# Cross attention on one Trainium2 core: four key tiles of each softmax denominator added by accumulating DMAs instead of by TensorE

## What is computed

```python
q = hidden_state @ Wq + bq                     # (b, 8, 4, l, 32)
k = encoder_hidden_state @ Wk + bk             # (b, 8, s, 32)
v = encoder_hidden_state @ Wv + bv
scores = einsum('bkgld,bksd->bkgls', q, k) * scale + mask
attn = softmax(scores, axis=-1)
out = einsum('bkgls,bksd->bkgld', attn, v)
x = out @ Wo + bo + hidden_state
return (x - mean(x)) * rsqrt(var(x) + EPS) * gamma + beta
```

## Time and profile before

| | |
|---|---|
| median of 3 runs | 4496.38 us (4492.47 to 4497.11) |
| profiled execution | 4489.78 us |
| its span, first to last instruction | 4488.1 us |
| busy in the span | TensorE 95%, VectorE 60%, GpSimd 59%, ScalarE 50% |
| mean granted TensorE clock | 0.973 |
| `attend` | about 853 to 4023 us |

### The profile page before, as it was taken

The page is one execution under the profiler, slowest core; times in us unless marked ns, Lnnn a source line. Parts: engine busy times, 40 slices in busy tenths (PEclk is TensorE's granted clock), DMA queues, the critical chain, the costliest instruction groups (busy, mean ns, idle before and its releaser), DMA issues. The chain is left out here.

```text
span 4488.1 us, 82254 instructions
## 1 busy us (share of the span) xinstructions
PE 4262.9 (95%) x26418; PEld 2461.2 (55%) x26418; DVE 2677.2 (60%) x4874; ACT 2259.2 (50%) x3861; POOL 2654.7 (59%) x857
## 2 busy tenths in 40 slices
PE   8999997999999999999999999999999999987887
PEld 7998885444444444444444444444444444436766
DVE  3344443766666666666666666666666666625555
ACT  2222111366666666666666666666666666651110
POOL 1111111377767777777677767776777777762444
PEclk9999998799999999999999999999999999998999
DMA  4445554211211212121221112112211211016553
GB/s 169 145 152 190 202 195 165 68 35 35 77 39 36 64 36 52 36 64 36 49 60 43 37 47 68 36 35 50 67 35 36 77 40 35 21 45 180 157 154 117
DMA packets 253832, 357.34 MB, mean 80 GB/s; under 512 B 123232, under 2 KB 160480, under 8 KB 253408
## 3 DMA queue, kind: packets, MB, share of 16 engines
q1 hardware_dynamic: 227920, 272.37, 22.1%
q0 software_dynamic: 21504, 70.80, 4.1%
q10 hardware_dynamic: 3984, 8.91, 0.5%
HBM read 262.35 MB, written 88.60 MB: 78 GB/s over the span
## 5 line engine op out<-in xcount | busy, mean ns | idle before, releaser
L871 ACT ACTIVATE weights<-logit 128x512 f32<-128x512 f32 (+1 forms) x3328 | 1974.4, 598 | 1156.2 <-PE logit L714 1139.2
L652 POOL TENSOR_TENSOR sum_pool<-sum_pool,weights 128x2048 f32<-128x2048 f32 x448 | 2057.1, 4592 | 303.1 <-ACT weights L871 287.5
L714 PE MATMUL logit<-q_sb,k_sb 98*128 98x512 f32 (+1 forms) x3328 | 1447.2, 439 | 35.7 <-issue 32.7
L825 DVE CUSTOM_DVE_ANT_0 masked_row<-score,mask_max,half_max 128x804 f32<-128x804 f32 x1024 | 1080.0, 1055 | 582.3 <-PE score L687 516.8
L825 DVE CUSTOM_DVE_ANT_0 masked_row<-score,mask_max 128x800 f32<-128x800 f32 x1024 | 1013.9, 990 | 420.3 <-PE score L687 306.4
L687 PE MATMUL score<-k_sb,q_sb 96*128 96x400 f32 (+1 forms) x4096 | 1158.9, 365 | 28.9 <-DVE half_max L825 10.2
L714 PEld LDWEIGHTS logit<-q_sb,k_sb 98*128 98x128 f32 (+1 forms) x3328 | 615.2, 185 | 759.6 <-ACT weights L871 636.3
L724 PE MATMUL mixed<-weights,v_sb 128*32 128x256 f32 (+1 forms) x10752 | 1001.2, 444 | 0.0
L687 PEld LDWEIGHTS score<-k_sb,q_sb 96*128 96x128 f32 x4096 | 754.2, 194 | 395.9 <-issue 154.9
L652 POOL TENSOR_TENSOR sum_pool<-weights 128x2048 f32<-128x2048 f32 x64 | 294.5, 4601 | 601.5 <-ACT weights L871 601.5
L724 PEld LDWEIGHTS mixed<-weights,v_sb 128*32 128x32 f32 x10752 | 212.1, 108 | 414.1 <-issue 396.5
(11 more groups left out here) (85 smaller groups left out, 2912.3 us busy)
## 6 DMA issues: line engine op xcount, KB each, us to landing
q_sb<-q_parts SPq DMA_DIRECT2D x192, 256.0 KB, 4.0
k_sb<-k_parts SPq DMA_DIRECT2D x192, 200.1 KB, 5.2
rows<-in_ctx SPq DMA_DIRECT2D x26, 1024.0 KB, 5.2
landing<-in_mask_Bx1xSxS_ff SPq DMA_DIRECT2D x32, 800.5 KB, 5.2
mask_max<-in_mask_Bx1xSxS_ff SPq DMA_DIRECT2D x32, 800.5 KB, 6.4
rows<-in_x SPq DMA_DIRECT2D x16, 1024.0 KB, 5.4
q_parts<-o_hi POOLq DMA_DIRECT2D x64, 256.0 KB, 2.3
q_parts<-o_lo POOLq DMA_DIRECT2D x64, 256.0 KB, 3.0
```

Of the source, the lines that this page charges most:

```text
L652: nc.gpsimd.tensor_tensor(sum_pool[s % 2][:], first[:], weights[buffer(s, st)][:], ALU.add).then_inc(pool_added, 1)
L714: last = nc.tensor.matmul(bank[0:w, :], k_sb[s][:, keys], q_sb[s][:, h, :], start=True, stop=not masked, skip_group_check=masked)
L825: nc.vector.tensor_tensor_reduce(masked_row[j][:].rearrange("p (c s) -> p c s", c=2), score[j][:, :, 0:w], mask_max[:, lt, s0:s0 + 2 * w]. ...
L871: nc.scalar.activation(weights[buffer(s, st)][0:w, h, :], logit[h % 2][0:w, :], ACT.Exp).then_inc(exp_done, 1)
```

## The change

GpSimd still adds its nine tiles. The four REST tiles are added into one of them by DMA: tile 2's buffer is the base, and tiles 5, 11 and 12 are added into it by `pool.dma_start(..., accum_op=ALU.add)`, issued by GpSimd in `add_rest` and counted by `rest_added`. The DMA of tile 5 is issued before the addition of tile 7 (n = 4), that of tile 11 before the addition of tile 10 (n = 7), so GpSimd waits there for tile 11's exponentials first; that of tile 12 after the addition of tile 10. Each waits for the one before it to land, the first for the mix of tile 2. `total` is gone. `denominators` sums `sum_pool`, waits for the third DMA, and sums the base, in one visit at tile 2 of the following step.

`sum_pool` has one buffer, so the first addition of a step waits until the step before's visit is over. Tile 2 has two buffers of its own, tiles 5, 11 and 12 have a ring of two. ScalarE waits for the DMA that read a buffer (tile 2: for the visit that read it) before it writes it anew. `EARLY` goes from 3 to 1, so two more slices of Wo, 512 KB each, are fetched by the output stage.

```diff
-EARLY = 3
+EARLY = 1
...
+    BASES = 2
...
+    ADD_REST = {4: 1, NPOOL - 1: 2}
...
-        sum_pool = [sb(f"sum_pool{i}", [P, G, LQ]) for i in range(2)]
+        weights = [sb(f"weights{i}", [P, G, LQ]) for i in range(BASES + sum(RINGS))]
+        sum_pool = sb("sum_pool", [P, G, LQ])
...
                 if n == 0:
-                    pool.wait_ge(denom_done, step + 1)
+                    pool.wait_ge(denom_done, step + 2)
...
+            def add_rest(quad, s, k):
+
+                step, st = quad * QUAD + s, REST[k]
+                w = min(P, S - st * P)
+                pool.wait_ge(exp_done, quad * (QUAD * ST * G) + (s * ST + st + 1) * G)
+                if k == 1:
+                    pool.wait_ge(mix_done, quad * (QUAD * ST) + (s * ST + REST[0] + 1 + MIX0))
+                else:
+                    pool.wait_ge(rest_added, step * 48 + 16 * (k - 1))
+                pool.sem_inc(pool_seen, 1)
+                pool.dma_start(weights[buffer(s, REST[0])][0:w], weights[buffer(s, st)][0:w], accum_op=ALU.add).then_inc(rest_added, 16)
...
                         for n in range(NPOOL):
+                            if n in ADD_REST:
+                                add_rest(a * (KVH // QUAD) + q, s, ADD_REST[n])
                             add(a * (KVH // QUAD) + q, s, n)
+                        add_rest(a * (KVH // QUAD) + q, s, 3)
...
-            def total(quad, tile):
-
-                s, st = tile // ST % QUAD, tile % ST
-                if st == REST[0] and not (isinstance(quad, int) and quad * QUAD + s == 0):
-                    pe.wait_ge(denom_copied, quad * QUAD + s)
-                pe.wait_ge(exp_done, quad * (QUAD * ST * G) + (tile + 1) * G)
-                w = min(P, S - st * P)
-                sum_heads(denom, ones[0:w, :], weights[buffer(s, st)], w, st == REST[0], False)
-
-            def denominators(step, par):
+            def denominators(quad, s):
+                step = quad * QUAD + s
+                if not (isinstance(step, int) and step == 0):
+                    pe.wait_ge(denom_copied, step)
                 pe.wait_ge(pool_added, step * NPOOL + NPOOL)
-                sum_heads(denom, ones[:], sum_pool[par], P, False, True).then_inc(denom_done, 1)
+                sum_heads(denom, ones[:], sum_pool, P, True, False)
+                pe.wait_ge(rest_added, step * 48 + 48)
+                sum_heads(denom, ones[:], weights[buffer(s % QUAD, REST[0])], P, False, True).then_inc(denom_done, 1)
...
                                 if st == SUMS_AT and not (first and s == 0):
-                                    denominators(quad * QUAD + (s - 1), (s - 1) % 2)
-                                if (tile - LAG) % ST in REST and not (first and tile < LAG):
-                                    total(quad, tile - LAG)
+                                    denominators(quad, s - 1)
```

More of the change, by code:

```diff
@@ L445, in ring @@
     def ring(st):
-        return (POOL, RINGS[0], 0) if st in POOL else (REST, RINGS[1], RINGS[0])
+        return (POOL, RINGS[0], BASES) if st in POOL else (REST[1:], RINGS[1], BASES + RINGS[0])
     def buffer(s, st):
+        if st == REST[0]:
+            return s % BASES
         tiles, size, first = ring(st)
@@ L454, in tile_before @@
     def tile_before(s, st):
+        if st == REST[0]:
+            return s - BASES, st
         tiles, size, _ = ring(st)
@@ L477, in attend @@
         parts_t = sb("parts_t", [NROW, 2, P], F32R)
-        weights = [sb(f"weights{i}", [P, G, LQ]) for i in range(sum(RINGS))]
-        sum_pool = [sb(f"sum_pool{i}", [P, G, LQ]) for i in range(2)]
+        weights = [sb(f"weights{i}", [P, G, LQ]) for i in range(BASES + sum(RINGS))]
+        sum_pool = sb("sum_pool", [P, G, LQ])
         ones = sb("ones", [P, HD])
@@ L510, in attend @@
         pool_added = sem("pool_added")
+        rest_added = sem("rest_added")
+        pool_seen = sem("pool_seen")
         mix_done = sem("mix_done")
@@ L650, in add @@
                     pool.wait_ge(pool_added, step * NPOOL + n)
-                    first = sum_pool[s % 2]
-                nc.gpsimd.tensor_tensor(sum_pool[s % 2][:], first[:], weights[buffer(s, st)][:], ALU.add).then_inc(pool_added, 1)
+                    first = sum_pool
+                nc.gpsimd.tensor_tensor(sum_pool[:], first[:], weights[buffer(s, st)][:], ALU.add).then_inc(pool_added, 1)
+            def add_rest(quad, s, k):
[8 more added lines that the diff above has]
+                pool.dma_start(weights[buffer(s, REST[0])][0:w], weights[buffer(s, st)][0:w], accum_op=ALU.add).then_inc(rest_added, 16)
             pool.wait_ge(flag_done, 1)
@@ L789, in steps @@
                 for tile in range(QUAD * ST - LAG, QUAD * ST):
-                    total(NQUAD - 1, tile)
                     mix(NQUAD - 1, tile)
-                denominators(NSTEP - 1, 1)
+                denominators(NQUAD - 1, QUAD - 1)
             pe.wait_ge(flag_done, 1)
@@ L863, in exponents @@
                 if h == 0 and not (isinstance(quad, int) and quad == 0 and before < 0):
-                    act.wait_ge(mix_done, quad * (QUAD * ST) + (before * ST + old + 1 + MIX0))
-                    if old in POOL:
-                        act.wait_ge(pool_added, quad * (QUAD * NPOOL) + (before * NPOOL + max(POOL.index(old), 1)))
+                    if st == REST[0]:
+                        act.wait_ge(denom_done, quad * QUAD + (before + 1 + 2))
+                    else:
+                        act.wait_ge(mix_done, quad * (QUAD * ST) + (before * ST + old + 1 + MIX0))
+                        if old in POOL:
+                            act.wait_ge(pool_added, quad * (QUAD * NPOOL) + (before * NPOOL + max(POOL.index(old), 1)))
+                        else:
+                            act.wait_ge(rest_added, quad * (QUAD * 48) + (before * 48 + 16 * REST.index(old)))
                 act.wait_ge(logit_done, quad * (QUAD * ST * G) + (n + 1 + LOGITS0))
```

## The result

The changed kernel takes 4953.70 us (median of 4 runs, 4952.83 to 4957.47) against 4496.43: a ratio of 1.102, 95% interval 1.100 to 1.104. It is slower, as forecast, but by 457 us and not 124, and outside the range.

What follows compares the result with a forecast made beforehand. TensorE, busy 95% of the span, was taken as the bound. 50 steps at +3.0 us (+152), 13 loop turns (-36), stage end (+5) and Wo (+3) gave +124, so 4620 us; range 4280 to 4850.

Steps and rivals of the forecast that it cites:

- TensorE saves 3.46 us a step: TensorE's matmuls: four denominator visits removed save 4.36 us, a second run of 8 matmuls costs 0.90, net 3.46 a step.
- The DMAs are issued at 19.2 and so on: GpSimd's queue, from tile 6's addition: tile 11's DMA issued at 19.2 us; TensorE wants tile 12's landed at 28.8.
- An accumulate takes twice the moving time: Accumulating DMAs: two reads double the moving part, so landing takes 7.1 us for tile 11 and 5.0 for tile 12.
- What DMA 11 meets: Tile 11's DMA beside the q and k loads: 5.5 us of movement becomes 10.5 if the two share evenly.
- DMA 12, 65 rows: Tile 12's accumulating DMA: 5 rows for each engine, 1.7 us as a copy, doubled, landing after 5.0 us alone.
- What it meets: Tile 12's DMA beside other traffic: 0.9 us for what is left of the loads and for v, if all pass in turn.
- Alone: Tile 12's DMA without the loads: issued at 26.4 us, landing at 31.4, which is 2.6 late.
- The lateness of 5.0 us: TensorE's wait for tile 12's DMA at tile 2: between 2.6 late alone and 8.5 with all in turn, taken as 5.0.
- The stall costs 1.5 us more by the clock: TensorE behind a stall of 5 us: the clock falls to 0.50, as behind a loop turn, losing 1.5 us.
- The 13 steps at a turn: Turns of the quad loop: GpSimd has 4.3 us more room, slow clock already paid; -3.46 + 0.7, 13 times: -36 us.
- The end of the stage and Wo: Stage end: tile 12's DMA behind the last addition, +5 us; output stage: 1 MB more of Wo, +3 us.
- My rival of 8.5 us late: Tile 2 wait: all DMAs pass in turn, or a slower accumulate; 8.5 us late, 4840 us; chance 0.20.

## Why the prediction was right in direction and wrong in size

- *TensorE saves 3.46 us a step.* 3.07: the count of the visits was right, and 0.4 goes to the wait for VectorE at tile 1. The statement that VectorE has room and doesn't take the place of the bound was true of the mean and not of that one place. Over the run it is 205 us, not 221.
- *The DMAs are issued at 19.2 and so on.* DMA 11 at 19.4; an accumulating issue takes 0.87 us of GpSimd, not 0.6, but only some of it in the chain. TensorE wants DMA 12 at 29.5, not 28.8.
- *An accumulate takes twice the moving time: DMA 11 7.1 us alone.* 7.0 without the loads. Right. The Trainium skill, Collectives: The Full Stack, on why ReduceScatter is half of AllGather, lays the half rate of an adding transfer to its two reads. DMA 5, which the loads of q, k and v don't reach, nearly agrees: its packets take 0.33 us as plain copies and 0.64 as accumulates, and its moving 3.2 and 5.4.
- *What DMA 11 meets.* It was down 9.6 us after its issue, as GpSimd sees it (29.0 less 19.4), where my middle value was 9.1. Right.
- *DMA 12, 65 rows: 5 rows for each engine, 1.7 us, doubled, lands after 5.0 alone, and 0.4 of 0.9 us more for what it meets: 5.4.* **This is the step that failed.** It took 9.0 us (2090.82 to 2099.83), and it is both terms that were wrong. *What it meets:* in 46 of 64 steps it stands behind the loads, which DMA 11 had held up, and moves its first byte after 4.4 us, not after 1.4: 3.0 us where I had 0.4. Its moving then takes 3.8, near my 3.4. *Alone:* 8.5 and not 5.0, because it starts at once but moves at half rate; rows 0 to 63 against 32 to 95 showed it, 7.9 to 4.4. I divided rows by engines and took the rate of transfers that span all the partitions. In the changed kernel this second term shows in few steps, above all those at the turns and the last ones, and it is why taking the loads away doesn't make DMA 12 land sooner. How much rows in the middle would gain beside the loads no run shows.
- *The lateness of 5.0 us.* 8.5 in the mean of the 50 steps that are not at a turn. DMA 12 took 3.6 more than forecast; its late issue (0.6) and TensorE's later wish for it (0.7) cancel.
- *The stall costs 1.5 us more by the clock.* The second term mis-sized: 2.3 in the mean of these 50 steps, up to 2.9. The stall of 8.5 us is over three times that of the loop's turn from which I took the price; in the step shown the clock is still at 0.50 some 6 us after work has begun again.
- *The 13 steps at a turn: 0.7 us of wait and no clock.* 5.3 of wait and 1.9 of clock. The wait is 3.2 less than in the other steps, where I allowed 4.3 less; in these steps DMA 12 moves at about half rate. And the clock, up again after the turn, falls once more behind the stall.
- *The end of the stage and Wo.* At the end of the stage TensorE waits 6.5 us for `sum_pool` and 8.2 for the DMA, where it waited 2.6: 12 us more, and I had 5. From the end of attention on the kernels take 465 and 464 us; `EARLY` costs nothing that can be seen, where I had 3.

Of the 333 us that the forecast was short, 50 steps make 215 (3.5 and 0.8 each), the turns 84, the saving 16 and the end of the stage 7, less 3 for Wo: 319.

The step shown adds up: 45.88 without DMAs, 8.54 of stall and 2.92 of clock are 57.34; the trace has 57.24 (2042.59 to 2099.83). Over the run this kernel takes 665 us more than the one without DMAs. Of these 501 are waiting, and the clock behind the stalls, 2.2 in the mean of 63 steps, makes 139 of the 164 left; the last 25 I can't assign. My rival of 8.5 us late gave 4840 and comes nearest, partly by luck: its lateness was right and it had DMA 12 behind what is left of the loads, but it gave DMA 11 12.1 us and DMA 12 5.9, where they took 9.6 and 9.0. What it lacks is mostly the clock (50 times 0.8) and the turns (13 times 3).

## What to carry to other kernels

Work moved off the bounding engine pays only if the wait that comes with it has room where it lands: here the same traffic went with a loss of 457 us or a gain of 191, by the tile at which the result was asked for. Ask of a short DMA not only how many bytes it moves, but what it stands behind and which partitions it touches, and measure each of the two: here taking away one brought out the other. And price a stall by what the clock costs behind one of its own length, not behind a shorter one.

## What the runs showed of the hardware that I had not expected

- With no loads about, a DMA of 64 rows of 8 KB, SBUF to SBUF with add, lands after 7.9 us from partitions 0 to 63, after 4.4 from 32 to 95, and one of 128 rows after about 7.
- The 8 KB packets of GpSimd's queue and the 2 KB ones of SyncE's take turns: while DMA 11 starts its 128 packets, 109 of 2 KB start (median of the steps). So the queue with the larger packets moves about four times the bytes: q's load went from 4.0 to 8.8 us to landing, the accumulate from 7.0 to 9.2.
- Beside the loads, DMA 12 moved its first byte 4.4 us after its issue and then moved in 3.8 us; without them it started after 1.4 and moved in 6.8. Why the late start goes with the full rate stays open.
- A turn of the loop took 2.6 us, and 5.5 where a DMA had been issued 2.4 us before it. The packets of kind `instruction` that start 0.3 to 1.6 us into the gap before the change start 5.1 to 5.4 us into it there. That they are held up by the DMA is shown by moving it; by what means they are held up is not.
